# Twenty-two groups, one load of constants, matrices ahead of tokens, and turned token tiles spread over a block in a fused FFN kernel

## The reference, cut to what matters

```
# layer 0, conditioning: each sequence picks one of 8 matrices (ids are 3 to 7 here)
w = weight[adapter_ids];  y = einsum('bsi,boi->bso', x, w)
# layer 0, feed-forward, added to x
h = relu(y @ up_w)**2;  shared = h @ down_w
moe = (y @ fc1_w @ expert_w) * sum(top2(y @ gate_w));  routed = moe @ fc2_w
x = x + layernorm(shared + routed)
# layer 1: LoRA-MLP conditioning and LoRA mixture
# layer 2, conditioning: q, k, v with norm and rope, attention over a paged cache, output
# layer 2 mixture, layer 3: untouched
```

## Time and profile before

| what | value |
|---|---|
| median of 3 runs | 3305.37 us (3300.33 to 3305.65) |
| profiled execution | 3301.96 us, of which the span is 3300.2 us |
| busy share | PE 97%, DVE 76%, ACT 56%, POOL 48% |
| mean granted clock of PE | 0.991 |
| l0_cond | 0 to 96.8 us |
| l0_ffn | 96.8 to 369 us |
| start of l2_attn | 1593.1 us |

### The profile page before, as it was taken

The page is one execution under the profiler, slowest core; times in us unless marked ns, Lnnn a source line. Parts: engine busy times, 40 slices in busy tenths (PEclk is TensorE's granted clock), DMA queues, the critical chain, the costliest instruction groups (busy, mean ns, idle before and its releaser), DMA issues. The chain is left out here.

```text
span 3300.2 us, 69952 instructions
## 1 busy us (share of the span) xinstructions
PE 3200.5 (97%) x21922; PEld 2950.0 (89%) x21922; DVE 2502.5 (76%) x6393; ACT 1859.0 (56%) x4601; POOL 1587.5 (48%) x2657
## 2 busy tenths in 40 slices
PE   6799999999999999999899999999999999999999
PEld 5677899988888888888899999999999999888887
DVE  6445644445577788878899999989999999688886
ACT  4323322233347778788666666656666666655533
POOL 0231000000017878888677777767777777144102
PEclk9899999999999999999999999999999999999999
DMA  5413423334555555556776776766777767888763
GB/s 209 143 60 73 132 82 82 87 109 142 204 172 184 173 169 182 177 185 198 248 245 236 238 239 236 242 200 231 243 237 236 239 236 249 309 294 310 280 198 112
DMA packets 406730, 645.38 MB, mean 196 GB/s; under 512 B 43289, under 2 KB 275545, under 8 KB 389466
## 3 DMA queue, kind: packets, MB, share of 16 engines
q1 hardware_dynamic: 386650, 502.49, 45.6%
q0 software_dynamic: 19712, 138.42, 12.6%
HBM read 440.74 MB, written 200.02 MB: 194 GB/s over the span
## 5 line engine op out<-in xcount | busy, mean ns | idle before, releaser
L2781 PE MATMUL l2a_x<-l2a_pt,l2a_V 128*128 128x128 f32 x4096 | 542.4, 275 | 2.6 <-issue 1.3
L2781 PEld LDWEIGHTS l2a_x<-l2a_pt,l2a_V 128*128 128x128 f32 x4096 | 498.5, 192 | 3.8 <-issue 3.8
L2693 DVE CUSTOM_DVE_ANT_0 l2a_sm<-l2a_s,l2a_B 128x544 f32<-128x544 f32 x512 | 367.0, 717 | 72.3 <-PE l2a_s L199 66.7
L2647 ACT ACTIVATE l2a_p<-l2a_sm,l2a_st 128x544 f32<-128x544 f32 x512 | 380.5, 743 | 45.3 <-DVE l2a_st L2693 42.1
L2473 POOL CAST keys<-cache 128x256 fp32r x750 | 301.4, 449 | 188.2 <-issue 155.5
L2632 ACT ACTIVATE l2a_pt<-l2a_t 128x512 f32<-128x512 f32 x512 | 304.1, 594 | 89.3 <-PE l2a_t L2764 85.6
L2705 DVE TENSOR_SCALAR l2a_p<-l2a_p,l2a_st 128x512 f32<-128x512 f32 x512 | 304.9, 596 | 18.2
L2473 POOL CAST l2a_K<-cache 128x256 fp32r x768 | 305.3, 445 | 16.7 <-issue 16.7
L2764 PE MATMUL l2a_t<-ident,l2a_p 128*128 128x128 f32 x2048 | 307.9, 273 | 5.2 <-ACT l2a_quads L2640 5.2
L2640 ACT ACTIVATE l2a_quads<-l2a_x 128x128 f32<-128x128 f32 x512 | 142.1, 278 | 278.3 <-PE l2a_x L2782 278.3
L2196 POOL MEMSET l2q_eps<- 128x5 f32 x1 | 0.1, 104 | 601.7 <-DMA s_x<-moe_xr 601.7
(11 more groups left out here) (1040 smaller groups left out, 8969.4 us busy)
## 6 DMA issues: line engine op xcount, KB each, us to landing
s_qT<-l2q_qo SPq DMA_DIRECT2D x128, 512.0 KB, 2.9
part<-s_ao SPq DMA_DIRECT2D x28, 2048.0 KB, 9.7
head<-s_qT SPq DMA_DIRECT2D x64, 512.0 KB
l2a_Q<-s_qT SPq DMA_DIRECT2D x64, 512.0 KB
s_ao<-l2a_combos SPq DMA_DIRECT2D x64, 512.0 KB
s_kn<-l2q_ko SPq DMA_DIRECT2D x128, 128.0 KB, 2.9
head<-s_kn SPq DMA_DIRECT2D x32, 512.0 KB, 5.8
s_ao<-l2a_quads SPq DMA_DIRECT2D x64, 256.0 KB, 2.2
```

The lines of the kernel that those rows point to most:

```text
L2647: act.activation(prr[sc % 6][:, :].rearrange("p (k g j) -> p g k j", k=4, j=8), smr[sc % 2][:, :].rearrange("p (g k j) -> p g k j", k=4, j ...
L2693: dve.tensor_tensor_reduce(out=smr[sc % 2][:, :], in0=ps_s[sc % 2][:, 224:768], in1=Br[g % 2][:, :], scale=-SCALE, scalar=3e38, op0=ALU.ad ...
L2781: pe.matmul(px[:, P:256], V[:, k * D + hg * P:k * D + hg * P + P], pt[:, k, :], start=k == 0, stop=False)
```

## The change

In l0_cond: the place of a sequence is 3 times its matrix number plus its rank, so 22 groups do. Four constants (`iota`, `icol`, `m4`, `m16`) come in one array `fixed`; `pcol` and `ident` are issued by ACT. The first four matrix tiles are issued ahead of the tokens, and ACT and DVE split them before they gather tokens. PE runs idle products while it waits, and takes all three passes of k = 0 for the first eight groups, then for k = 1, 2, 3 the high and the low passes in turn. The first three up tiles of l0_ffn are loaded during l0_cond, over the tokens' room, when those have been read, and ACT splits off their high parts there.

In l0_ffn: SP waits for the fourth gathered tile before it issues the further weights; gamma and beta come after those. POOL no longer splits up tile 2; DVE does, ahead of the token tiles. PE starts with idle products. In blocks 1 and 2 the turns of the next block stand one each behind up products 1, 3, 5 and 7; in block 0 they stay behind the gate. The rows' transposition stands behind the first down product.

In l2: `iota` and the new keys of the first sequence are prepared in l2_qkv; in l2_attn DVE waits for the last stores after its first mask, the late half of the chunk follows the first scoring unit, and POOL gathers values before it clears two tiles.

```diff
-    NG = NB // 4 + 7
+    NG = NB // 4 + 6
+    fixed, fixed_in = S["quarters"][2][0:NB, 0:P + NT + 1 + NL], st.sem("fixed")
...
-            sp.dma_start(iota[:, :], A["iota544"][0:NB, 0:NL]).then_inc(iota_in, 16)
-            sp.dma_start(icol[:, :], A["icol"][0:NB, :]).then_inc(icol_in, 16)
-            sp.dma_start(m4[:, :], A["m4"]).then_inc(m4_in, 16)
-            sp.dma_start(m16[:, :], A["m16"]).then_inc(m16_in, 16)
-            sp.dma_start(pcol[:, :], A["pcol"]).then_inc(pcol_in, 16)
+            sp.dma_start(fixed, A["fixed"]).then_inc(fixed_in, 16)
+            matrices(range(4))
             for k in range(4):
                 sp.dma_start(xs[:, k, :], A["xT"][k * P:(k + 1) * P, :]).then_inc(x_in[k], 16)
+            matrices(range(4, 16))
             for s in range(NG):
                 sp.wait_ge(copied, s + 1)
                 sp.dma_start(S["y0"][s * P:(s + 1) * P, :], y[s][:, :]).then_inc(y.sem(s), 16)
+                if s == NG - 7:
+                    sp.wait_ge(x_lo, 4 * NG)
+                    for k in range(3):
+                        sp.dma_start(early[k].unsqueeze(1), rows_of(A["up"], k, 1)).then_inc(S["up_in"][k], 16)
...
+            act.dma_start(pcol[:, :], A["pcol"]).then_inc(pcol_in, 16)
+            act.dma_start(ident[:, :], A["ident"]).then_inc(ident_in, 16)
...
+            weights(0)
             act.wait_ge(tabled, 1)
             for k in range(4):
                 act.wait_ge(x_in[k], 16)
-            high(0)
-            weights(0)
-            for s in range(1, 8):
+            for s in range(8):
                 high(s)
...
+            for k in range(3):
+                act.wait_ge(S["up_in"][k], 16)
+                act.activation(S["up_high"][:, k, :], early[k], ACT.Copy).then_inc(S["up_hi"], 1)
...
-            dve.scalar_tensor_tensor(val[:, 5:6], val[:, 1:2], 4.0, val[:, 4:5], ALU.mult, ALU.add).then_inc(*steps.mark())
+            dve.scalar_tensor_tensor(val[:, 5:6], val[:, 1:2], 3.0, val[:, 4:5], ALU.mult, ALU.add).then_inc(*steps.mark())
...
+            weights(0)
             dve.wait_ge(tabled, 1)
-            low(0)
-            for s in range(1, 8):
+            for s in range(8):
                 low(s)
-            for k in range(4):
+            for k in range(1, 4):
                 weights(k)
...
+            pe.wait_ge(ident_in, 16)
+            keep_busy(pe, banks[6][:, 0:P], ident[:, :], 16)
+            pe.wait_ge(x_in[1], 16)
+            keep_busy(pe, banks[6][:, 0:P], ident[:, :], 20)
+            pe.wait_ge(x_in[3], 16)
+            keep_busy(pe, banks[6][:, 0:P], ident[:, :], 8)
+            pe.wait_ge(w_lo, 4)
+            for s in range(8):
+                pe.wait_ge(x_lo, 4 * s + 4)
+                group(s, 0, (0, 1, 2), first=True)
+            for k in range(1, 4):
                 pe.wait_ge(w_hi, 4 * k + 4)
                 for s in range(8):
-                    if k == 0:
-                        pe.wait_ge(x_lo, 4 * s + 4)
-                    group(s, k, (0, 1), first=k == 0)
-            for k in range(4):
+                    group(s, k, (0, 1))
                 pe.wait_ge(w_lo, 4 * k + 4)
                 for s in range(8):
                     i = group(s, k, (2,), last=k == 3)
...
+    def next_turns(cb, u):
+        if cb == 3:
+            return ()
+        return [4 * cb + 4 + j for j in range(4) if ((1, 3, 5, 7) if cb else (10, 10, 10, 10))[j] == u]
...
+            sp.wait_ge(*front.nat.landed(3))
             for m in range(8):
                 for k in extra(m):
                     w.fetch(sp, k)
+            sp.dma_start(gam[:, :], row_bc(A["gamma"], D)).then_inc(gam_in, 16)
+            sp.dma_start(bet[:, :], row_bc(A["beta"], D)).then_inc(bet_in, 16)
...
-            w.low(pool, 2)
...
-            w.low(dve, 0)
-            w.low(dve, 1)
-            for t in range(4):
+            for k in range(3):
+                w.low(dve, k)
+            front.low(dve, 0)
+            w.low(dve, 3)
+            for t in range(1, 4):
                 front.low(dve, t)
-            w.low(dve, 3)
...
-            pe.wait_ge(ident_in, 16)
+            keep_busy(pe, pw[0][:, 0:P], ident[:, :], 20)
...
+                    for t in next_turns(cb, m):
+                        front.turn(pe, t)
...
-                bank_free(pe, 22 * cb + 13)
-                pe.wait_ge(row_copied, 4 * cb + 4)
-                pe.transpose(bank(cb, 13)[:, 0:P], rows[:, :], ident[:, :]).then_inc(row_turned, 1)
...
                     if t == 0:
+                        bank_free(pe, 22 * cb + 13)
+                        pe.wait_ge(row_copied, 4 * cb + 4)
+                        pe.transpose(bank(cb, 13)[:, 0:P], rows[:, :], ident[:, :]).then_inc(row_turned, 1)
                         pe.wait_ge(lat_lo, 2 * cb + 2)
...
+                    sp.dma_start(S["iota"][0][:, :], A["keypos"]).then_inc(S["iota"][1], 16)
...
+                if n == 7 * NT + 6:
+                    dve.wait_ge(kn0_in, 16)
+                    dve.tensor_copy(K0[:, 16, :, :].rearrange("p z (h s) -> p h z s", h=4), kn0[:, :, :, 0:32]).then_inc(S["keyed"], 1)
...
-            new_keys(0)
-            dve.wait_ge(chunk_hi, 1)
-            low_part(dve, [z[:, late, :] for z in chunk_tiles(3)], st0[:, late, :]).then_inc(chunk_v, 1)
             dve.wait_ge(iota_in, 16)
             mask(0)
+            for q in S["qkv_stores"]:
+                for k in range(8 * NT - 2, 8 * NT):
+                    dve.wait_ge(*q.landed(k))
```

More of the change, by code:

```diff
@@ L259, in l0_cond @@
     ident, ident_in = S["ident"]
+    early = [S["ring"][:, 1024 * k:1024 * k + 1024] for k in range(3)]
     def w_tile(w, q):
@@ L492, in l0_ffn @@
                  (gw[:, :, 0:8], gw[:, :, 8:16], rows_of(A["gw"], 0, 4))] +
-                [part(down, "down", 2 * k, 2) for k in range(4)], bufs=lead.ring)
+                [part(down, "down", 2 * k, 2) for k in range(4)], own=3, bufs=lead.ring, sems=S["up_in"])
+    w.hi = S["up_hi"]
     front = Front(st, S["y0"], ident, 4, lambda t: sl(yT[t // 4 % 2], S_, S_, slice(t % 4 * P, (t % 4 + 1) * P)),
@@ L642, in _ @@
         def _(act):
-            for k in range(3):
-                w.high(act, k)
+            w.high(act, 3)
             for t in range(4):
                 front.high(act, t)
-            w.high(act, 3)
             for cb in range(4):
@@ L667, in _ @@
                         w2.high(act, m)
+                    for t in next_turns(cb, m):
+                        front.high(act, t)
                 for m in range(2):
@@ L672, in _ @@
                     act.activation(lat[0][:, m, :], bank(cb, 8 + m)[:, :], ACT.Copy).then_inc(lat_hi, 1)
+                    for t in next_turns(cb, 8 + m):
+                        front.high(act, t)
                 act.wait_ge(gate_mm, cb + 1)
@@ L679, in _ @@
                     act.activation(rows[32 * t:32 * t + 16, :], bank(cb, 10)[0:16, t * P:(t + 1) * P], ACT.Copy).then_inc(row_copied, 1)
-                if cb < 3:
-                    for t in range(4 * cb + 4, 4 * cb + 8):
-                        front.high(act, t)
-                else:
+                for t in next_turns(cb, 10):
+                    front.high(act, t)
+                if cb == 3:
                     for t in range(2):
@@ L781, in _ @@
                         w2.low(dve, m)
+                    for t in next_turns(cb, m):
+                        front.low(dve, t)
                 for m in range(2):
@@ L842, in _ @@
                 i.then_inc(gate_mm, 1)
[L843 to L848 removed]
+                if cb == 0:
+                    pe.wait_ge(ex_lo, 2)
+                for t in next_turns(cb, 10):
+                    front.turn(pe, t)
+                if cb == 3:
                     for t in range(2):
                         tokens.turn(pe, t)
[L851 to L853 removed]
                 for t in range(4):
@@ L2695, in _ @@
                     if sc == 0:
+                        dve.wait_ge(chunk_hi, 1)
+                        low_part(dve, [z[:, late, :] for z in chunk_tiles(3)], st0[:, late, :]).then_inc(chunk_v, 1)
                         chunk_done(dve, 3)
```

67 lines of the change are left out of this document (30 added, 37 removed).

## The result

The changed kernel takes 3283.81 us as the median of four runs (3282.46 to 3284.62), the kernel before 3303.44 us in its four runs beside it: a ratio of 0.994, with a 95% interval of 0.9928 to 0.9953. It is 19.6 us faster. The profiled execution took 3282.46 us, its span is 3280.7 us, 19.5 less than before.

A forecast was written before the change was run, and what follows sets the result against it. PE was busy 97% of the span, with DVE bounding the first eight groups. Terms 4.9 + 2.7 + 4.5 + 2.5 + 3.6 + 0 + 0.8 = 19.0 us gave 3283.0 (profiled) or 3286.4 (median), taken as 3285; range 3277 to 3296.

The forecast's parts named there:

- First eight groups: l0_cond: earlier loads and matrix tiles ahead of tokens start group 8 at 49.4 instead of 54.26 us, -4.9 us.
- one group: l0_cond: one group fewer saves 12 products of 0.2275 us, all on PE's path, -2.7 us.
- Between the stages: From l0_cond's end to l0_ffn's first up product: shorter gather landings and moved subtractions save 4.5 us.
- T + 13.9: Forecast start of l0_ffn's first up product, T being PE's end in l0_cond; before the change it was T + 18.45.
- the 0.5 added for DVE's subtractions: Between the stages: 0.5 us allowed for the fourth gather, as gathers beside DVE's subtractions took longer to issue.
- The clock: Start of l0_ffn: idle products keep PE's clock high, so the first up product is faster, -2.5 us; the least certain term.
- if the clock lasts: Condition at l0_ffn's start: the first up product then takes 2.7 us instead of 5.3; if not, nothing is gained.
- first rival: The clock falls between the idle products and the turns at l0_ffn's start: gain 16.0 us, time 3288, chance 0.27.
- Spread turns: l0_ffn blocks 1 and 2: turns spread over up products remove two waits of PE, -3.6 us; block 0 keeps its wait.
- the rows' transposition: l0_ffn: moving it behind the first down product gains PE nothing, 0 us, with bounds +1 to -0.4.
- Start of l2_attn: PE starts at once instead of after 3.83 us idle; only its shift counts, -0.8 us, bounds 0 to -1.5.
- what hides the move's own effect on DVE: l0_ffn: DVE's first sum comes 1.3 us later, but the lag shrinks over four tiles and vanishes in the next up products.

The follow-up runs named there:

- e3: Changed kernel with tokens loaded and split ahead of all matrices again, and PE's high passes of all four k before the low ones: 3285.96 us.
- e1: Changed kernel with 23 groups and places of 4 again instead of 22 and 3: 3286.08 us.
- e7: Changed kernel without SP's wait for the fourth gathered tile, so further weights load beside the gathers again: 3288.57 us.
- e11: Changed kernel itself run again, unedited, on one chip beside the kernel before (3304.12 us): 3285.55 us.
- e5: Changed kernel with 26 idle products instead of 20 ahead of l0_ffn's first turn, and 1, 2, 4, 5 behind the four turns: 3284.10 us.
- e6: Changed kernel with the rows' transposition ahead of the first down product again, turns still spread: 3286.41 us.
- e2: Changed kernel with the next block's four turns together behind the gate in blocks 1 and 2 again, rows' transposition still moved: 3288.68 us.
- e10: Changed kernel with block 0's tiles 4 and 5 turned behind up products 1 and 3, split ahead of weights, plus idle products between the front turns: 3288.88 us.
- e12: Changed kernel with block 0's tiles 4 and 5 turned behind up products 1 and 2, split ahead of weights, plus idle products between front turns: 3280.68 us.

## Why the prediction was right

The time, 3283.8 against 3285, and the sum, 19.5 against 19.0, were right. Not all terms were, and that the sum came so close is in part luck: the six terms forecast gave 18.0 us, and 1.4 us of the rest come from layer 1, where the clock happened to be low in the kernel before's profiled execution (0.63) and high in this one (1.00).

- **First eight groups and one group** were right to 0.1 us, and e3 and e1 show why. With the tokens first, DVE's row of splits ends at 49.61 and sets the start of group 8 (52.19); in the changed kernel it ends at 45.16, and PE goes on to 49.43 without a wait for it. A group is all PE.
- **Between the stages** the sum was right (T + 13.85 against T + 13.9). The fourth gather started 4.1 us behind the first (95.49 and 91.41), 3.9 before, so 0.2 of the 0.5 added for DVE's subtractions was paid. The last link was another than forecast: the fourth turn waited 1.05 us for DVE's low part of the second tile and not for a landing. e7 shows that the bulk loads beside the gathers were the main part; POOL's and DVE's moved subtractions were not tried apart.
- **The clock** was the mis-sized term: 2.5 forecast, 0.8 in one execution (4.46 us from the first to the second up product instead of 5.26), and nothing by e11 (5.28). The step "if the clock lasts" failed. Idle products that end at 94.0 do not carry it over turns with 0.3 to 1.7 us between them; over the first up product it was 0.61 in the mean. The prediction's first rival, that the clock is lost ahead of the up products, was right in e11, where the clock fell during the turns; in the first execution it fell only inside the first up product, and the turns ran at 1.00. e5 shows a form of it in which the clock lasts.
- **Spread turns and the rows' transposition**: the sum, 4.6 us over three blocks, beat the 3.6, but the split into "-3.6" and "0" failed. e6 (spread, not moved) takes 177.69 us for the three blocks, the kernel before 178.57, the changed kernel 173.96: spreading alone gives 0.9. Moving alone gives nothing where the turns stand together (e2, second row), and about 0.7 in the third row, where there are none to spread (57.24 against 57.98 and 57.99). The other 3.0 us come only from both together. The prediction named what hides the move's own effect on DVE, and that was right (the first sum is 8.6 us behind its down product, 1.4 later than before, and nothing waited). It missed that the removed turns were themselves the cover of the row copies in blocks 1 and 2. So the move is what makes the spreading pay.
- **Start of l2_attn** gave 0.4 instead of 0.8, within its bounds; PE's start was then released by the stage's start, 3.38 us behind PE's last work. No run takes this part of the change back, and none the early loads of the up tiles.
- Three amounts outside the sum are -0.7 in block 0, -2.0 in layer 1 and +1.3 elsewhere. Of the first, 0.3 is the tail of the low clock behind 119.08 in the kernel before (its second up product's first two matmuls took 0.74 us against 0.47), and 0.3 a shorter wait for the expert matrices' low part (1.1, now 0.8). Of the second, 1.4 us are the mixture's clock, which is chance (e11). Of the third, 0.5 is the wait at layer 1's start (2.2 us, 1.7 in the earlier trace rows), where DVE ends last, as the prediction said. The rest was not traced.

By the medians the change is worth 19.6 us here and 18.6 beside e11, whose span is 18.3 us shorter than the kernel before's.

## What to carry to other kernels

Ask of work that is moved away what waited unseen beneath it: two edits that give little alone (0.9 and about 0.7 us) gave 4.6 us together. Behind a full row of splits on ACT and DVE, where a tile's split stands in that row decides, not where PE turns it. And in a stretch of small steps, idle products between all of them, sized by the gaps in the trace, kept the clock up in three kernels of three; idle products ahead of the stretch alone did not.

## What the runs showed of the hardware

- A wait of 1.5 or 1.8 us between dense stretches took the clock to about 0.50 for some 2.5 and 3.4 us (an estimate from the clock of the windows) behind two of e2's three blocks of turns, and behind none of the kernel before's, whose waits are as long. The Trainium skill ("TensorE: Matmul & The Clock Gate", "Why this matters for your kernels") warns of idle gaps between bursts; e5, e10 and e12, without such gaps, agree with it.
- A gather takes POOL 0.95 us to issue, but 1.70 us beside DVE's subtraction of two SBUF tiles (97.65), 1.60 so in the kernel before, and 0.95 beside one that reads a bank (96.73, 101.24). The first gather of the stage took 1.11 us with DVE idle and 1.26 beside such a subtraction (89.32). The Trainium skill ("SBUF - State Buffer", "Who interferes with whom") infers that such a subtraction does not meet the writing of descriptors; these rows speak against that, and the measurement decides.
- Two weight tiles of 512 KB beside the gathers raised the median landing from 4.0 to 5.1 us and moved the first up product by 3.2.
